# Query projections moved to slot 6, the SyncE queue and batch 0's jobs reordered, in a macaron attention block

## The reference

```python
x = x + 0.5 * ffn(layernorm(x))                 # ffn: fft, sparse complex weights, inverse fft, bias
x = x + attn(layernorm(x), Wq, Wk, Wv, Wo, bo)  # 16 heads of 8, on the left 128 channels
x = x + 0.5 * ffn(layernorm(x))
# attn: q, k, v = left @ W.T ; softmax(q k^T / 4) v ; @ Wo.T + bo
```

## Time and profile before

| | us |
|---|---|
| median of 3 executions | 317.19 |
| lowest, highest | 316.79, 319.31 |
| the profiled execution, its own time | 320.35 |
| span of the instructions in it | 318.5 |

### The profile page before, as it was taken

The page is one execution under the profiler, slowest core; times in us unless marked ns, Lnnn a source line. Parts: engine busy times, 40 slices in busy tenths (PEclk is TensorE's granted clock), DMA queues, the critical chain, the costliest instruction groups (busy, mean ns, idle before and its releaser), DMA issues.

```text
span 318.5 us, 8826 instructions
## 1 busy us (share of the span) xinstructions
PE 298.2 (94%) x3445; PEld 113.4 (36%) x3449; DVE 189.6 (60%) x550; ACT 259.3 (81%) x287; POOL 97.7 (31%) x112
## 2 busy tenths in 40 slices
PE   8888899899999999999997999899998999998985
PEld 5644333233333333333332333233332333222333
DVE  1687535758775778477863778367854653360264
ACT  2215989998998989898996989798998999999921
POOL 6734701043604251404504251403500340034014
PEclk9999999999999999999999999999999999999999
DMA  7835572146456364825474363625461564112102
GB/s 202 312 134 196 204 285 115 58 160 240 138 184 221 134 199 141 290 105 200 133 224 176 134 201 117 184 101 199 136 203 66 185 214 165 38 68 66 36 33 68
DMA packets 26564, 49.86 MB, mean 157 GB/s; under 512 B 2065, under 2 KB 14737, under 8 KB 24721
## 3 DMA queue, kind: packets, MB, share of 16 engines
q1 hardware_dynamic: 25824, 48.78, 44.4%
q10 hardware_dynamic: 688, 0.40, 0.7%
HBM read 31.34 MB, written 17.83 MB: 154 GB/s over the span
## 4 chain that ended last, share of the span: by engine, by line
PE 66%; DMA 11%; DVE 10%; issue 6%; ACT 5%; POOL 1%; SPq 1%; PEldq 0%; ACTq 0%; DVEq 0%
PE misc L715 24%; PE ot L823 24%; PE scores L795 12%; DMA QS<-q_scr 9%; ACT probs L665 5%; DMA left_scr<-left_blocks 3%; PE scores L682 2%; DVE left_blocks L963 2%; PE scores L715 1%; PE scores L689 1%; DVE kp L982 1%; DVE lh L954 1%; DVE kp L980 1%; DVE stats L936 1%; DVE VS L1027 1%
## 5 line engine op out<-in xcount | busy, mean ns | idle before, releaser
L665 ACT ACTIVATE probs<-scores 128x1024 f32<-128x1024 f32 x256 | 243.9, 1029 | 25.6 <-PE scores L795 22.7
L823 PE MATMUL ot<-probs,VS 128*32 128x512 f32 x1024 | 134.4, 594 | 3.9 <-ACT probs L665 2.9
L795 PE MATMUL scores<-QS,KS 32*128 32x512 f32 x512 | 64.8, 495 | 5.7 <-DMA QS<-q_scr 5.0
L795 PEld LDWEIGHTS scores<-QS,KS 32*128 32x128 f32 x512 | 24.5, 181 | 112.8 <-ACT probs L665 100.3
L1014 DVE SCALAR_TENSOR_TENSOR x_out<-misc,rstd,x_out 128x256 f32<-128x256 f32 x28 | 13.6, 484 | 48.2 <-PE misc L715 44.8
L823 PEld LDWEIGHTS ot<-probs,VS 128*32 128x32 f32 x1024 | 30.8, 109 | 28.0 <-ACT probs L665 7.1
L558 POOL TENSOR_TENSOR x_out<-x,half_bias 128x512 f32<-128x512 f32 x7 | 9.0, 1290 | 92.4 <-DVE x L1009 92.4
L543 POOL TENSOR_SCALAR veps<-mv 128x4 f32<-128x4 f32 (+1 forms) x25 | 5.7, 227 | 96.4 <-DVE mv L943 96.4
L715 PE MATMUL misc<-half_ffn,xT 128*32 128x256 f32 x448 | 33.1, 387 | 0.0
L715 PE MATMUL misc<-half_ffn,xT_in 128*32 128x256 f32 x400 | 27.9, 385 | 1.8 <-DVE half_ffn L1185 1.3
L545 POOL TENSOR_TENSOR rstd<-veps,power 128x4 f32<-128x4 f32 (+1 forms) x25 | 25.2, 1008 | 2.1
(11 more groups left out here) (126 smaller groups left out, 259.3 us busy)
## 6 DMA issues: line engine op xcount, KB each, us to landing
KS<-k_scr SPq DMA_DIRECT2D x14, 512.0 KB, 4.5
QS<-q_scr SPq DMA_DIRECT2D x14, 512.0 KB, 4.5
x_in<-x SPq DMA_DIRECT2D x8, 512.0 KB, 6.4
xT_in<-x_t SPq DMA_DIRECT2D x8, 512.0 KB, 7.3
k_scr<-kp SPq DMA_DIRECT2D x8, 512.0 KB, 2.8
q_scr<-qp SPq DMA_DIRECT2D x8, 512.0 KB, 3.7
x_scr<-x_blocks SPq DMA_DIRECT2D x7, 512.0 KB, 3.5
xT<-x_scr SPq DMA_DIRECT2D x7, 512.0 KB, 4.5
```

Source lines behind the costliest of these rows:

```text
L665: nc.scalar.activation(probs[u % PRING][:, :, :], scores[u % SRING][:, :, :], ACT.Exp, scale=SCORE_SCALE).then_inc(exp_done, 1)
L795: last = mm(scores[(u + j // 2) % SRING][:, j % 2, :], KS[b % 2][rows, slot, kt * P:(kt + 1) * P].bitcast(F32R), QS[b % 2][rows, slot, :]. ...
L823: last = mm(ot[COL * j:COL * (j + 1), :], VS[b % 2][:, kt, h, :], probs[(u + j // 2) % PRING][:, j % 2, :], start=s % 8 == 0, stop=s % 8 == 7)
```

## The change

Batches 1 to 5 do both query jobs in slot 6 (`QT_0` left, `QT_1` right) and move `F1_3` from slot 6 to slot 7, `V_0` to slot 8 and `V_1` to slot 9. VectorE's `left_half` of these batches moves one slot later, from slots 8 and 9 to slots 9 and 10; ScalarE's square of the queries moves ahead of slot 9 for all batches after batch 0 and to slot 10 in batch 0. SyncE issues a batch's loads of x after the store of the second output half and not before it, and both loads of the query rows ahead of the left half, no longer around it. In batch 0 the jobs are interleaved in another order.

```diff
-          6: [("F1_3a", 2, LEFT), ("F1_3", 2, LEFT)], 7: [("QT_0", 1, LEFT)], 8: [("QT_1", 1, LEFT)],
-          9: [("V_0", 1, RIGHT), ("V_1", 1, LEFT)], 10: [("N", 1, RIGHT), ("F2_0a", -1, LEFT)], 11: [("F2_0", -1, LEFT)],
+          6: [("QT_0", 1, LEFT), ("QT_1", 1, RIGHT)], 7: [("F1_3a", 2, LEFT), ("F1_3", 2, LEFT)],
+          8: [("V_0", 1, RIGHT)], 9: [("V_1", 1, LEFT)], 10: [("N", 1, RIGHT), ("F2_0a", -1, LEFT)], 11: [("F2_0", -1, LEFT)],
...
-BEGIN = {1: [("LT", 1, LEFT)], 2: [("KT_0", 1, LEFT), ("KT_1", 1, RIGHT)], 3: [("QT_0", 1, LEFT), ("QT_1", 1, RIGHT)],
-         4: [("F1_0a", 2, LEFT), ("F1_0", 2, LEFT)], 5: [("F1_1a", 2, LEFT)], 6: [("F1_1", 2, LEFT), ("F1_2a", 2, RIGHT)],
-         7: [("F1_2", 2, RIGHT)], 8: [("F1_3a", 2, LEFT), ("F1_3", 2, LEFT)], 9: [("V_0", 1, RIGHT)],
-         10: [("V_1", 1, LEFT), ("N", 1, RIGHT)]}
+BEGIN = {1: [("LT", 1, LEFT)], 2: [("KT_0", 1, RIGHT), ("F1_0a", 2, LEFT)], 3: [("F1_0", 2, LEFT), ("KT_1", 1, RIGHT)],
+         4: [("F1_1a", 2, LEFT)], 5: [("F1_1", 2, LEFT), ("QT_0", 1, RIGHT)], 6: [("F1_2a", 2, LEFT)],
+         7: [("F1_2", 2, LEFT), ("QT_1", 1, RIGHT)], 8: [("F1_3a", 2, LEFT), ("F1_3", 2, LEFT)],
+         10: [("N", 1, RIGHT)], 11: [("V_0", 1, RIGHT)], 12: [("V_1", 1, LEFT)]}
...
             for it in range(1, B):
+                if it >= 2:
+                    store_out(it - 2, 1)
                 if it + 3 < B:
                     load_x(it + 3)
-                if it >= 2:
-                    store_out(it - 2, 1)
...
                 if it + 1 < B:
                     q_out(it + 1)
+                    q_in(it + 1)
                 if it + 2 < B:
                     left_through(it + 2)
-                if it + 1 < B:
-                    q_in(it + 1, slice(0, 1))
-                if it + 2 < B:
                     leftT_in(it + 2)
-                if it + 1 < B:
-                    q_in(it + 1, slice(1, None))
                 store_out(it - 1, 0)
...
-                    if s == (2 * (8 if it == B - 2 else 10) if it else 2 * 7):
+                    if s == (2 * 9 if it else 2 * 10):
                         square(qp, sq_q, qp_step, it + 1)
...
-                        if s == (8 if it else 10):
+                        if s == (9 if it else 10):
                             left_half(it + 2, range(0, 2))
-                        if s == (9 if it else 11):
+                        if s == (10 if it else 11):
                             left_half(it + 2, range(2, T))
                             turn_left(it + 2)
```

## The result

| | before | after |
|---|---|---|
| median, us | 318.12 | 323.17 |
| lowest to highest of 4 | 316.79 to 319.31 | 322.68 to 323.37 |
| the profiled execution, its own time | 320.35 | 323.37 |
| its span | 318.5 | 321.6 |

The ratio is 1.0156, with a 95% interval of 1.0122 to 1.019: the changed kernel is slower, by 1.6%.

What follows compares the result with a forecast made beforehand. TensorE and ScalarE were taken to have no slack in batches 1 to 5. Profiled: 320.35 - 5.8 + 2.8 + 3.5 + 4.2 - 0.4 = 324.7 us; median forecast 323.3, range 318.0 to 325.3.

Steps and rivals of the forecast that it cites:

- The boundary waits go: At batch boundaries, TensorE's late starts for query rows vanish because the rows load earlier: -5.8 us, bounds -5.8 and -2.6.
- The fifth piece: Before batch 2, a value group followed after 1.48 instead of 0.97 us; this 0.51 was counted among the boundary savings.
- the second choice: Carrying the profiled time to the median: 321.5 if the 3.16 lead is fixed, 324.7 if boundary waits; 323.3 taken.
- the 2.6 of the prediction: At batch boundaries, the us of waits that before's median would hold if the profiled execution's lead is those waits.
- The pair, +2.8: Slot 7's F1_3a job waits for two query halves evacuated in slot 6: 0.56 us in each of five batches.
- take_values behind F1_3, +3.5: Slot 8's values wait for VectorE's transposition of ot, queued behind F1_3 and its statistics: 0.7 us in five batches.
- left_half behind the norms' chain, +4.2: Slot 12's job waits for F2_0's evacuation, delayed by the later left_half and turn: 0.85 us in five batches.
- The left half in time: Left half, turned later, lands at 168.4 before the next batch's first key job at 170.9: no cost.
- Batch 0, -0.4: Batch 0's reordered jobs lose two 0.56 us waits and gain smaller ones: net -0.4 us, bounds -1.1 and +0.5.
- The sum: Whole kernel, profiled execution: 320.35 us plus all terms gives 324.7 us.
- The forecast's signs: In batches 1 to 5: waits of about 0.5, 0.6 to 0.7 and 0.8 us at slots 7, 8, 12; even 36.5 us batches.
- The rival on the other side: Slack in TensorE's half-job slots absorbs the stalls, only boundary waits go: median 311 to 314.2 us, chance 0.11.

Runs made afterwards that it cites:

- experiment 8: Kernel before with only batch 0's new job order and its square of the queries ahead of slot 10: 316.95 us, 0.9938 of before.
- experiment 1: Kernel before with only both query-row loads issued ahead of the left half: 315.61 us, 0.9946 of before.
- experiment 2: Kernel before with both queue edits, query rows ahead of the left half and x's loads behind the second output half's store: 315.21 us, 0.9932 of before.
- experiment 9: Kernel before with both queue edits and batch 0's new order, old tables for batches 1 to 5: 314.58 us, 0.988 of before.
- experiment 10: Kernel before with both queue edits and both query halves in slot 7, V_0 in 8, V_1 in 9, F1_3 left in 6: 318.33 us.
- experiment 6: Changed kernel with slot 7's take_values placed between F1_3's evacuation and its statistics: 320.33 us, 1.0066 of before.
- experiment 5: Changed kernel with left_half back in slots 8 and 9: 319.97 us, 1.0047 of before.
- experiment 3: Changed kernel with both queue edits taken back, so the old SyncE order: 337.59 us, 1.067 of before.
- experiment 4: Kernel before with only left_half one slot later, in slots 9 and 10: 329.98 us, 1.041 of before.

## Why the prediction was right

**The boundary waits go: right.** The four with the query rows as their releaser, 5.0 us by TensorE's waits, are gone. The fifth piece, 0.51 us ahead of batch 2, went too, but no row ties it to the query rows: the scores ahead of it at 97.82 had come without a wait, and nothing is named as the releaser of the pause in the value group. In experiment 8, with the old queue and a boundary wait at that very place, there was no such pause. Its 0.5 us in the -5.8 came out right without a shown cause.

**The carry to the median, the second choice.** How much the median of before held of the boundary waits was left open. The changed kernel's profiled execution is 0.20 above its median; the one of before was 3.16 above the median it was compared with. So the lead of 3.16 is no fixed cost of profiling. It goes with the boundary waits: experiment 8, which still has 4.1 us of them, was profiled 1.9 us above its median, and experiments 1 and 2, without them, 0.4 above and 0.7 below. The changed kernel's four executions lie within 0.7 us, those of the kernel before within 2.5. Experiment 1 removes the waits and gains 1.6 us of median, experiment 2 gains 2.0. Other executions of before held more: experiment 9, less batch 0's 0.6, gains 3.2 on the 318.4 of its group, and the 5.05 us between the two medians of the result, set against the 8.9 us of the four terms below, leave 3.8. So before's median held between 1.6 and 3.8 us of them, varying by group; the 2.6 of the prediction lies inside.

**The pair, +2.8: measured 5 x 0.57 = 2.85.** Its twin in batch 0 was as exact as could be asked, and experiment 10 moves it with the pair.

**take_values behind F1_3, +3.5: measured 5 x 0.63 = 3.15,** and 2.8 when undone in experiment 6. Mechanism right, size a little high: from F1_3's evacuation to the transposition 1.48 us passed and not 1.56, since the transposition starts 0.08 us before the row of the aggregates ends (157.36 and 157.06 + 0.38 = 157.44). Starts, not ends, were to be subtracted. Against the 1.91 us that slot 8 took in before the cost is 0.58 a batch, 2.9 in five.

**left_half behind the norms' chain, +4.2: measured 5 x 0.71 = 3.55,** and 3.2 when undone in experiment 5. The term was too large by 0.14 a batch: from the chain's start to F2_0's evacuation 165.42 - 162.20 = 3.22 us passed where 1.58 + 1.76 = 3.34 were taken, and the evacuation itself read 0.45.

**The left half in time: right.** Its load went out at 167.62 and its first key job began at 174.24.

**Batch 0, -0.4: measured -0.66** (from the first scores of slot 0 to those of batch 1: 65.22 - 31.82 = 33.40 before, 64.87 - 32.13 = 32.74 after), and 0.6 by experiment 9. The 0.17 at slots 4, 6 and 8 are there. The term was a quarter of a microsecond too small.

**The sum.** 320.35 - 5.8 + 2.85 + 3.15 + 3.55 - 0.66 = 323.4, against 323.37 measured; of two small things left out, a start 0.31 us later and short waits of 0.05 us in before's slot 8 that went, one makes up for the other. The forecast of 324.7 for this execution was 1.3 high, by three of the terms above. That the 323.3 for the median lies within 0.2 us of the 323.17 measured is luck in part: the terms were 1.3 too high in sum, and the choice between the two carries took 1.4 off. With the right terms and the right carry (no fixed lead) it would have been 323.4. The forecast's signs all came: the three waits in five batches, 36.3 us a batch where 36.5 was said, and values of slot 8 that begin 1.49 us after the scores.

**The rival on the other side** asked whether TensorE's half-job slots have slack of their own. They have none that shows: experiments 5 and 6 each take one wait out, and each of the five batches is shorter by 0.71 and 0.58 us, the full length of that wait. The medians fell by 3.2 and 2.8.

## What to carry to other kernels

Where two engines alternate with no slack, an evacuation's price is not its length but its place: list the consumer's due times, and count the producer's instructions ahead of each. Moving a transfer's source earlier is worth nothing while its issue stands in a queue behind something that is late; change the queue first, on its own. A wait's size can be read from a twin elsewhere in the trace, and durations are best taken from start to start.

## What the runs showed of the hardware

A wait can cost more than its length. In experiments 3 and 4 TensorE waited five times each for the rows, 10.9 and 11.2 us, and the granted clock fell behind two of the waits in experiment 3 and behind one in experiment 4. Stretches of experiment 3:

```profile
core 0: us, PE busy (x) PEld busy (x) DVE busy (x) ACT busy (x) POOL busy (x), PEclk, DMA share, GB/s
135.00:145.00 10.00, 7.99 (x78) 2.42 (x68) 2.97 (x10) 6.81 (x8) 3.72 (x4) 0.83 0.69 234
145.00:165.00 20.00, 18.99 (x236) 7.00 (x228) 14.44 (x40) 16.54 (x18) 7.55 (x8) 1.00 0.47 160
...
175.00:185.00 10.00, 7.60 (x88) 2.50 (x84) 4.12 (x13) 6.88 (x9) 3.71 (x4) 1.00 0.68 237
```

The first and the third both hold a boundary wait; in the first the mean clock was 0.83, that is part of the stretch at 1.2 GHz in place of 2.4, in the third it stayed at 1.00. The two slots behind the wait at 139.74 lost 0.54 + 1.03 = 1.6 us to it. The loss did not begin at once: from 140 to 141, with TensorE at work again, the granted clock was still 1.00, and from 141 to 144 it was 0.50. The length of the wait does not tell which one is followed by it. In experiment 3 the waits were 2.32, 2.01, 2.40, 1.78 and 2.43 us, and the clock fell behind the two shortest, 2.01 and 1.78; in experiment 4 it fell behind the longest of 2.42, 2.22, 2.02, 2.28 and 2.24. In before it stayed at 1.00 behind the 2.15 of the earlier trace rows. What decides it stays open; no run was made for it.

A transfer behind others pays for them. In experiment 1 the 256 KB store of the left half, issued right behind the two loads of query rows, took 5.71 us; in before, ahead of the second load, it took 2.00. The chain of waits of experiment 1:

```profile
189.47 5.33 DMA q_scr<-qp
...
196.08 5.71 DMA left_scr<-left_blocks
```

The late store made `leftT` late once, by 0.6 us: what the query rows gained in the queue was partly taken from the left half, which had it to spare in all batches but one.

A transfer can also be late with nothing beside it. The queries' own store in this chain took 5.33 us where the median of before was 3.7. The DMA engines had been idle from 189 to 190; from 190 to 192 they moved 254 GB/s, which is about the 512 KB of this store, and from 192 to 195 only 11 GB/s. So about three of the 5.33 us lie between the last of its bytes and its landing at 194.80, and the loads of the query rows waited for all of them. Why this store landed so late stays open.
